# Two cross-attention layers on one core: queries of two units projected together in every second slot, and the second layer's weights loaded in six parts

## The chip, the cores and the metric

The kernel runs on one core of one Trainium2 chip. The metric is the device time of one execution in microseconds (us). A measurement of this kernel scatters by about 0.1% between runs (1834.97 to 1836.72 us in three runs).

## What is computed

Two grouped-query cross-attention layers one after the other, each on 32 batch entries of 112 query rows and 375 context rows, width 512, with 32 query heads over 8 key/value heads of 16 columns each:

```python
q = hidden_state @ Wq + bq          # [32, 112, 512]
k = encoder_hidden_state @ Wk + bk  # [32, 375, 128]
v = encoder_hidden_state @ Wv + bv  # [32, 375, 128]
scores = jnp.einsum('bkgld,bksd->bkgls', q, k) * scale + mask
attn = jax.nn.softmax(scores, axis=-1)
out = jnp.einsum('bkgls,bksd->bkgld', attn, v)   # back to [32, 112, 512]
x = out @ Wo + bo + hidden_state
x = (x - mean(x)) * rsqrt(var(x) + EPS) * gamma + beta
```

The second layer takes the first one's x, and the same context.

## The kernel before

A **unit** is one batch entry in one layer, so there are 64. Units run in two lines, p = 0 and p = 1 (even and odd batch entries), and the program is a chain of **slots** (p, i), i from -1 to 33, in the order (0, i), (1, i), (0, i+1). A slot works on five units at different stages: the scores, exponentials and values of its own unit (`main`), the row maxima and value projection of the next one of the other line (`ahead`), the end of the one before (`post`: reciprocals, output projection), the key and query projection of the next unit of its own line (`proj`), and the layer norm and store of the last one of its own line (`stored`).

A slot has 12 **pieces** (k = 0 to 11). Every piece has one pair of score matmuls on TensorE (tile `sc`, L741) and their two exponentials on ScalarE (ACT, L500); a `sc` buffer is written again only when its exponential is done. The other work of a slot hangs on the piece number, on each engine, by hand. On TensorE these are: 16 pairs of matmuls for the row maxima (tile `ms`, L758; `PAIRS_AT` says how many in which piece, one right behind the scores and the second, if there is one, at the piece's end), the values in two halves (tile `pv`, L777), the projections of values (L795), keys (L807), queries (L841) and outputs, a head in each of four pieces (L819), the transpose of the result rows in layer 0 (L832), and twice the small matmul that turns the maxima into rows (L786). VectorE (DVE) reduces each pair of `ms` to maxima (L627); there are two `ms` buffers, so pair j waits until pair j-2 is reduced:

```python
if j >= 2:
    pe.wait_ge(max_done[o], PAIRS * ahead + j - 1)
```

The maxima become three bf16 parts on POOL (L428 to L434), are turned by L786 into the tile `job`, copied by ACT (`mT`, L519) and brought by a DMA on SP's queue (L310) into the rows of `qs` from which the scores subtract them; the scores of piece 0 and piece 6 wait for these rows. `job` is one PSUM bank that values' projection, maxima's rows, queries and outputs take in turn, each waiting for the evacuation of the one before. Queries are projected by 16 matmuls of 112 columns for each unit, evacuated by four activations (L556), split into three bf16 parts by ACT and POOL, and stacked by 12 DMAs into `qs`.

TensorE, ACT, DVE and POOL work in program order; all loads, stacking and stores but the outputs' are issued in order on SP's queue (`slot` under `block.sync`). The second layer's weights (10 DMAs) are issued there at the end of slot (1, 1).

## Time and profile before

| | |
|---|---|
| Time, median of 3 runs | 1835.99 us |
| The profiled execution's own time | 1835.3 us |
| Its span in the profile | 1833.2 us |
| PE (TensorE) busy | 1779.6 us, 97% |
| DVE busy | 1370.1 us, 75% |
| ACT busy | 1078.4 us, 59% |
| POOL busy | 571.0 us, 31% |
| DMA, mean | 129 GB/s |

The profile's engines are PE for matmuls, PEld for the loads of stationary operands, DVE, ACT, POOL, and SP and ACT as issuers of DMAs (SPq, ACTq). An fp32 matmul has two records, a bf16 matmul one. A busy PE says that matmuls are in flight, not that each goes at its best rate, so distances from one start to the next are read rather than durations.

### The profile page before, as it was taken

What the parts mean: (1) busy time and instruction counts of PE and PEld (TensorE: products, weight loads), DVE (VectorE), ACT (ScalarE), POOL (GpSimd) and SP (SyncE); (2) the same over time, 40 slices, a digit from 0 to 9 for tenths busy, and PEclk for the clock granted to TensorE, in tenths of its full rate; (3) what the DMA queues carried; (4) which work ended last, traced back from release to release, by engine and by line L of the source; (5) the groups of instructions that cost most, each with busy time, mean ns of one, the idle gap of its engine ahead of it and who ended that gap; (6) DMA issues with size and microseconds to landing.
All of it is one profiled execution on the core that took longest, in us unless ns stands there. A gap on an engine that the chain in (4) does not pass through costs nothing. (4 is left out here: it accounts for less than half of the span.)

```text
span 1833.2 us, 37386 instructions
## 1 busy us (share of the span) xinstructions
PE 1779.6 (97%) x11521; PEld 1153.3 (63%) x11521; DVE 1370.1 (75%) x1808; ACT 1078.4 (59%) x2530; POOL 571.0 (31%) x1165
## 2 busy tenths in 40 slices
PE   4899999999999999999999999999999999999996
PEld 3566566666666666666666666666666666666652
DVE  6577677777777777777777777787777777777784
ACT  1465565666656656656656656656665656656653
POOL 1232233323323323323323323323323333333321
PEclk8899899999999999999999999999999999999997
DMA  8346445445445445445445445444444444444431
GB/s 288 100 121 180 130 125 137 129 120 140 129 121 139 132 117 142 133 115 144 133 119 144 128 109 135 128 111 133 128 114 131 126 116 127 125 126 117 129 82 42
DMA packets 200894, 235.92 MB, mean 129 GB/s; under 512 B 41706, under 2 KB 176100, under 8 KB 199812
## 3 DMA queue, kind: packets, MB, share of 16 engines
q1 hardware_dynamic: 180356, 205.82, 40.0%
q10 hardware_dynamic: 20480, 29.38, 6.9%
q8 instruction: 31, 0.51, 0.1%
q14 instruction: 27, 0.22, 0.0%
HBM read 101.39 MB, written 22.02 MB: 67 GB/s over the span
## 5 line engine op out<-in xcount | busy, mean ns | idle before, releaser
L627 DVE TENSOR_REDUCE mx<-ms 112x2 f32<-112x750 f32 x1024 | 933.4, 933 | 412.6 <-PE ms L758 401.1
L500 ACT ACTIVATE probs<-sc 125x448 f32<-125x448 f32 x1536 | 751.5, 542 | 344.5 <-PE sc L741 337.0
L758 PE MATMUL ms<-ks,qs 96*112 96x375 bf16 x2048 | 501.0, 326 | 10.4 <-DMA qs<-qp 7.8
L741 PE MATMUL sc<-qs,ks 99*125 99x448 bf16 x1536 | 423.6, 356 | 11.1 <-DMA qs<-mT 8.3
L758 PEld LDWEIGHTS ms<-ks,qs 96*112 96x112 bf16 x2048 | 254.7, 131 | 223.5 <-issue 114.4
L777 PE MATMUL pv<-probs,vs 125*32 125x448 f32 x3072 | 317.4, 546 | 0.0
L741 PEld LDWEIGHTS sc<-qs,ks 99*125 99x125 bf16 x1536 | 199.5, 138 | 127.5 <-ACT probs L500 75.3
L819 PE MATMUL job<-wo,on 128*112 128x512 f32 x512 | 268.6, 607 | 7.2 <-POOL on L442 5.7
L841 PE MATMUL job<-xT,wq 128*128 128x112 f32 x2048 | 249.9, 276 | 0.0
L841 PEld LDWEIGHTS job<-xT,wq 128*128 128x128 f32 x2048 | 245.2, 193 | 3.5 <-issue 0.6
L456 POOL TENSOR_TENSOR kr<-kf,kp 128x375 f32<-128x375 f32 x64 | 57.5, 899 | 534.5 <-ACT kp L537 534.5
L642 DVE RECIPROCAL orec<-osum 128x112 f32<-128x112 f32 x256 | 214.8, 841 | 5.8 <-DMA osum<-oraw 5.8
L807 PE MATMUL pv<-ctxT,wk 128*128 128x375 f32 x512 | 185.3, 484 | 10.0 <-DMA bq<-in_bq 10.0
L795 PE MATMUL job<-wv,ctxT 128*125 128x128 f32 x1536 | 191.9, 276 | 0.0
L795 PEld LDWEIGHTS job<-wv,ctxT 128*125 128x125 f32 x1536 | 187.7, 191 | 4.1
L777 PEld LDWEIGHTS pv<-probs,vs 125*32 125x32 f32 x3072 | 87.3, 110 | 163.1 <-issue 162.5
L508 ACT COPY oraw<-pv 128x448 f32<-128x448 f32 x128 | 68.1, 532 | 166.7 <-PE pv L777 166.7
L807 PEld LDWEIGHTS pv<-ctxT,wk 128*128 128x128 f32 x512 | 96.2, 192 | 49.0 <-issue 11.7
L556 ACT ACTIVATE qf<-job,bqs 128x112 f32<-128x112 f32 x256 | 69.6, 354 | 89.0 <-PE job L841 89.0
L428 POOL TENSOR_TENSOR mwide<-mx,zero 112x16 bf16<-112x16 f32 x128 | 27.5, 215 | 279.1 <-DVE mx L627 271.5
L475 POOL TENSOR_TENSOR qp<-qr,qp 128x224 bf16<-128x224 f32 x128 | 75.2, 608 | 104.9 <-ACT qp L574 104.9
L819 PEld LDWEIGHTS job<-wo,on 128*112 128x112 f32 x512 | 82.8, 178 | 37.1 <-issue 17.6
(54 smaller groups left out, 999.1 us busy)
## 6 DMA issues: line engine op xcount, KB each, us to landing
ctxT<-in_ctxT SPq DMA_DIRECT2D x64, 750.0 KB, 5.8
qs<-qp SPq DMA_DIRECT2D x768, 56.0 KB, 2.7
ks<-kp SPq DMA_DIRECT2D x768, 46.9 KB, 2.5
osum<-oraw ACTq DMA_DIRECT2D x128, 112.0 KB, 2.8
oc<-oraw ACTq DMA_DIRECT2D x128, 112.0 KB, 3.4
mask<-in_mask SPq DMA_DIRECT2D x64, 164.1 KB, 2.3
xT<-in_xT SPq DMA_DIRECT2D x32, 224.0 KB, 6.5
xin<-in_x SPq DMA_DIRECT2D x32, 224.0 KB, 6.6
```

Source lines behind the costliest of these rows:

```text
L475: nc.gpsimd.tensor_tensor(qp[:, 2, cols], qr[:, cols], qp[:, 1, cols], ALU.subtract)\
L500: nc.scalar.activation(probs[0:KCS, k, j, :], sc[j][0:KCS, 0:GL], ACT.Exp)\
L556: nc.scalar.activation(qf[:, S * c:S * c + S], job[:, S * c:S * c + S], ACT.Identity, bias=bqs[lay[3]][:, c:c + 1], scale=SCALE).then_inc( ...
L627: nc.vector.tensor_reduce(mx[o][:, 2 * j:2 * j + 2], ms[j % 2][0:S, :, 0:S2], AX_X, ALU.max)\
L642: nc.vector.reciprocal(orec[:, S * n:S * n + S], osum[:, S * n:S * n + S])\
L741: last = nc.tensor.matmul(sc[j][0:KCS, 0:GL], ks[p][0:KM, g, rows], qs[p][0:KM, g, :], start=True, stop=not masked)
L758: last = nc.tensor.matmul(ms[j % 2][0:S, n, 0:S2], qs[o][0:KT, g, S * c:S * c + S], ks[o][0:KT, g, :], start=True, stop=True)
L777: last = nc.tensor.matmul(pv[32 * j:32 * j + 32, 0:GL], vs[u][:, chunk, 4 * h + j, :, :].rearrange("s d two -> s (d two)"), probs[0:KCS, H ...
L795: last = nc.tensor.matmul(job[0:KCS, P * c:P * c + P], ctxT[o][:, t, KCS * c:KCS * c + KCS], wv[lay[1]][:, t, :], start=(t == 0), stop=(t ...
L807: last = nc.tensor.matmul(pv[:, 0:S2], wk[lay[3]][:, t, :], ctxT[p][:, t, :], start=(t == 0), stop=(t == DC - 1))
L819: last = nc.tensor.matmul(job[0:S, 0:D], on[:, S * c:S * c + S], wo[lay[2]][:, c, :], start=(c == 0), stop=(c == NG - 1))
L841: last = nc.tensor.matmul(job[:, S * c:S * c + S], wq[lay[3]][:, t, c, :], xT[p][:, t, :], start=(t == 0), stop=(t == DC - 1))
```

## The change

The place of every piece of work is now in tables with one row for p = 0 and one for p = 1. Queries of both units of a pair (same i, both lines) are projected in the slot of p = 0, by 16 matmuls of 224 columns for two units in place of 16 of 112 for each; `xT` holds both units side by side, `job` takes two heads' groups at a time, and ACT evacuates both units in one activation each group. In the slot of p = 0 two of the four heads' output projections move to the first two pieces of the slot of p = 1. Values' first half and the turned maxima come later in p = 0 (pieces 8 and 9 for 7 and 7). The store of the transposed rows moves a slot on, `xT` is loaded for both lines in the slot of p = 1, and the second layer's weights are loaded in six parts in slots (0,0), (1,0), (0,1), (1,1), (0,14) and (1,14).

```diff
-PAIRS_AT = [2, 2, 1, 2, 0, 1, 1, 1, 2, 2, 1, 1]
+PAIRS_AT = [[1, 1, 1, 1, 1, 1, 1, 2, 1, 2, 2, 2], [1, 1, 1, 1, 2, 1, 1, 1, 2, 2, 2, 1]]
+LATE_HEADS_AT = [{}, {0: (2,), 1: (3,)}]
+HEADS_AT = [{10: (0,), 11: (1,)}, {8: (0,), 9: (1,), 10: (2,), 11: (3,)}]
+KEYS_AT = [{2: (0,), 3: (1, 2), 4: (3,)}, {2: (0, 1), 3: (2, 3)}]
+VALUES_AT = [{1: (0, 1), 2: (2,)}, {4: (0, 1), 5: (2,)}]
+QUERIES_AT = [{4: (0,), 5: (1,), 6: (2,), 7: (3,)}, {}]
+COLUMNS_AT = [(9, 3), (7, 2)]
+FIRST_HALF_AT = [8, 7]
+RECIPROCALS_AT = [4, 4]
+WORK_FIRST = [(5,), (0,)]
...
-        xT = two(sb, "xT", [P, DC, S])
+        xT = sb("xT", [P, DC, PAR, S])
...
-                sp.dma_start(xT[p][:, :, :].rearrange("p a b -> p (a b)"), src[b]).then_inc(xT_in[p], 16)
+                sp.dma_start(xT[:, :, p, :], src[b].rearrange("p (a b) -> p a b", a=DC)).then_inc(xT_in[p], 16)
...
                     def project_queries(heads):
+                        if heads[0] % 2 == 0:
+                            take_job_bank()
                         if 0 in heads:
-                            take_job_bank()
-                            pe.wait_ge(xT_in[p], 16 * (proj + 1))
+                            for u in range(PAR):
+                                pe.wait_ge(xT_in[u], 16 * (proj + 1))
                         for c in heads:
                             for t in range(DC):
-                                last = nc.tensor.matmul(job[:, S * c:S * c + S], wq[lay[3]][:, t, c, :], xT[p][:, t, :],
+                                last = nc.tensor.matmul(job[:, PAR * S * (c % 2):PAR * S * (c % 2 + 1)], wq[lay[3]][:, t, c, :],
+                                                        xT[:, t, :, :].rearrange("p u l -> p (u l)"),
                                                         start=(t == 0), stop=(t == DC - 1))
...
+            def next_layer(p, i):
+                if (p, i) == (0, 0):
+                    load_wk(1, w_in[1])
+                    load_wv(1, w_in[1])
+                if (p, i) == (1, 0):
+                    load_wq(1, w_in[1], slice(0, 2))
+                if (p, i) == (0, 1):
+                    load_wq(1, w_in[1], slice(2, DC))
+                if (p, i) == (1, 1):
+                    load_wo(1, w_in[1], slice(0, 2))
+                if (p, i) == (0, PER - 2):
+                    load_wo(1, w_in[1], slice(2, NG))
+                if (p, i) == (1, PER - 2):
+                    load_rows(1, w_in[1])
```

Three places in the built programs. First TensorE, pieces 5 to 7 of a slot of p = 0 before the change: scores (L741), a pair for the maxima (L758), queries (L841) in two blocks of eight matmuls, and the transposes between.

```order
L741 MATMUL sc<-qs,ks 125x448 x2
L753 REGISTER_ALU
L758 MATMUL ms<-ks,qs 112x375 x2
L841 MATMUL job<-xT,wq 128x112 x8
L738 ISA
L741 MATMUL sc<-qs,ks 125x448 x2
L753 REGISTER_ALU
L758 MATMUL ms<-ks,qs 112x375 x2
L832 MATMUL pv<-ident,y 128x112 x4
L841 MATMUL job<-xT,wq 128x112 x8
```

The same engine at the same place of the changed program (scores L834, maxima L851, queries L937, transposes L925), from the end of piece 5 to piece 7:

```order
L937 MATMUL job<-xT,wq 128x224 x4
L846 REGISTER_ALU
L851 MATMUL ms<-ks,qs 112x375 x2
L831 ISA
L834 MATMUL sc<-qs,ks 125x448 x2
L846 REGISTER_ALU
L851 MATMUL ms<-ks,qs 112x375 x2
L925 MATMUL pv<-ident,y 128x112 x4
L822 ISA
L937 MATMUL job<-xT,wq 128x224 x4
```

Blocks of eight narrow matmuls became blocks of four matmuls twice as wide, one in each of pieces 4 to 7; the slot of p = 1 has none.

Second TensorE again, the changed program's pieces 8 to 10 of p = 0, with the values' first half (L870), the turned maxima (L879) and the first head of the output projection (L912):

```order
L870 MATMUL pv<-probs,vs 32x448 x12
L831 ISA
L834 MATMUL sc<-qs,ks 125x448 x2
L846 REGISTER_ALU
L851 MATMUL ms<-ks,qs 112x375 x2
L822 REGISTER_ALU
L878 ISA
L879 MATMUL job<-negident,mwide 128x112
L846 REGISTER_ALU
L851 MATMUL ms<-ks,qs 112x375 x2
L831 ISA
L834 MATMUL sc<-qs,ks 125x448 x2
```

Piece 9 now holds no projection between its scores and those of piece 10; before, the turned maxima stood right behind the values, and each of the pieces 8 to 11 had a head.

Third SP's queue, the end of slot (1, 1) before the change, with the ten loads of the second layer's weights in one go:

```order
L299 DMA yT_mid<-yT 128x448
L364 DMA wk<-in_Wk 128x512
L365 DMA bk<-in_bk 128x1
L368 DMA wq<-in_Wq 128x2048
L369 DMA bq<-in_bq 128x4
L372 DMA wv<-in_Wv 128x512
L361 DMA bv<-in_bv 125x128
L376 DMA wo<-in_Wo 128x2048
L361 DMA bo<-in_bo 112x512
L361 DMA gamma<-in_gamma 112x512
L361 DMA beta<-in_beta 112x512
```

And the middle of slot (1, 0) in the changed program, with one of the six parts:

```order
L330 DMA qs<-mT 3x16x112
L298 DMA xT<-in_xT 128x4x112 x2
L399 DMA wq<-in_Wq 128x1024
L308 DMA xin<-in_x 112x512
L325 DMA ks<-kp 16x4x375 x6
L285 DMA ctxT<-in_ctxT 128x1500
L325 DMA qs<-qp 16x4x448 x5
L330 DMA qs<-mT 3x16x112
```

The part stands behind the slot's first row of maxima (L330) and ahead of `xin`, the stacking of the keys and, in a slot of p = 1, the context, which moved behind the keys' stacking.

## Rows read from the trace of the kernel before

**Rows 1.** The page, busy time by engine (us, share, instructions)
```profile
PE 1779.6 (97%) x11521; PEld 1153.3 (63%) x11521; DVE 1370.1 (75%) x1808; ACT 1078.4 (59%) x2530; POOL 571.0 (31%) x1165
```

**Rows 2.** Timeline of PE in a layer-0 slot (start, length, line, operation, records)
```profile
804.64 0.55 PE L741 MATMUL sc<-qs,ks 99*125 99x448 bf16 x2
805.02 0.48 PE L758 MATMUL ms<-ks,qs 96*112 96x375 bf16 x2
805.52 1.11 PE L819 MATMUL job<-wo,on 128*112 128x512 f32 x2
806.46 0.49 PE L758 MATMUL ms<-ks,qs 96*112 96x375 bf16 x2
806.78 0.54 PE L741 MATMUL sc<-qs,ks 99*125 99x448 bf16 x2
807.16 0.48 PE L758 MATMUL ms<-ks,qs 96*112 96x375 bf16 x2
807.48 1.02 PE L819 MATMUL job<-wo,on 128*112 128x512 f32 x2
808.34 0.48 PE L758 MATMUL ms<-ks,qs 96*112 96x375 bf16 x2
...
816.04 1.91 PE L795 MATMUL job<-wv,ctxT 128*125 128x128 f32 x16
817.78 0.49 PE L758 MATMUL ms<-ks,qs 96*112 96x375 bf16 x2
...
824.37 1.94 PE L841 MATMUL job<-xT,wq 128*128 128x112 f32 x16
826.14 0.55 PE L741 MATMUL sc<-qs,ks 99*125 99x448 bf16 x2
```

**Rows 3.** Timeline of PE, values' first half (piece 7) of successive slots, layer 0
```profile
129.35 2.46 PE L777 MATMUL pv<-probs,vs 125*32 125x448 f32 x24
156.89 2.46 PE L777 MATMUL pv<-probs,vs 125*32 125x448 f32 x24
193.89 2.46 PE L777 MATMUL pv<-probs,vs 125*32 125x448 f32 x24
```

**Rows 4.** The same in layer 1
```profile
1240.47 2.46 PE L777 MATMUL pv<-probs,vs 125*32 125x448 f32 x24
1267.69 2.46 PE L777 MATMUL pv<-probs,vs 125*32 125x448 f32 x24
```

**Rows 5.** Timeline of ACT around the pieces 8 and 9 of Rows 2
```profile
804.71 0.53 ACT L508 COPY oraw<-pv 128x448 f32<-128x448 f32 x1 [0.46 <-PE pv L777]
805.14 0.24 ACT L519 CAST mT<-job 48x112 bf16<-48x112 f32 x1
...
807.17 0.54 ACT L500 ACTIVATE probs<-sc 125x448 f32<-125x448 f32 x1 [0.38 <-PE sc L741]
...
807.61 0.54 ACT L500 ACTIVATE probs<-sc 125x448 f32<-125x448 f32 x1
```

**Rows 6.** Timeline of DVE, the reduction behind the maxima's pair at 805.02
```profile
805.55 0.94 DVE L627 TENSOR_REDUCE mx<-ms 112x2 f32<-112x750 f32 x1 [1.56 <-PE ms L758]
```

**Rows 7.** Timeline behind the second layer's weight loads, SP's queue and PE
```profile
180.49 0.78 SPq L310 DMA_DIRECT2D qs<-mT  x1
...
187.55 1.00 PE L741 MATMUL sc<-qs,ks 99*125 99x448 bf16 x2 [6.61 <-DMA qs<-mT]
```

**Rows 8.** The page, DMA issues (count, KB each, median us from issue to landing)
```profile
ctxT<-in_ctxT SPq DMA_DIRECT2D x64, 750.0 KB, 5.8
qs<-qp SPq DMA_DIRECT2D x768, 56.0 KB, 2.7
...
xT<-in_xT SPq DMA_DIRECT2D x32, 224.0 KB, 6.5
```

**Rows 9.** Timeline of PE at the start, from the first maxima to the first scores
```profile
32.38 1.47 PE L758 MATMUL ms<-ks,qs 96*112 96x375 bf16 x4 [5.68 <-DMA qs<-qp]
...
55.45 1.01 PE L741 MATMUL sc<-qs,ks 99*125 99x448 bf16 x2 [1.32 <-DMA qs<-mT]
```

More of the change, by code:

```diff
@@ L327, in slot @@
                     max_rows(p, 1, count(2 * main + 2))
+                turned = stored if p == 1 else stored - 1
+                if not isinstance(turned, int) and lay[4] == 0 or isinstance(turned, int) and 0 <= turned < PER:
+                    store_yT(o, turned)
                 if s_ok:
                     store_y(p, stored, lay[4])
-                if more and not (isinstance(ahead, int) and ahead + 1 == 0):
-                    after = lay[3] if not isinstance(ahead, int) else 0 if ahead + 1 < PER else 1
-                    load_ctx(o, ahead + 1, after)
-                    load_xT(o, ahead + 1, after)
+                if p == 1 and (not isinstance(proj, int) or 0 < proj + 1 < UNITS):
+                    after = lay[3] if not isinstance(proj, int) else 0 if proj + 1 < PER else 1
+                    for u in range(PAR):
+                        load_xT(u, proj + 1, after)
+                if isinstance(i, int):
+                    next_layer(p, i)
+                if more and p == 0 and not (isinstance(ahead, int) and ahead + 1 == 0):
+                    load_ctx(o, ahead + 1, lay[3] if not isinstance(ahead, int) else 0 if ahead + 1 < PER else 1)
                 if m_ok:
@@ L384, in _ @@
             load_xT(0, 0, 0)
+            load_xT(1, 0, 0)
             for n in range(BLOADS):
@@ L519, in m_out, with k_out, q_out, rows_out @@
                     nc.scalar.copy(mT[:, :], job[0:PARTS * HH, 0:S]).then_inc(mt_evac[u], 1)
+                def k_out():
+                    act.wait_ge(k_ps[p], proj + 1)
+                    if a_ok:
+                        act.wait_ge(k_r[o], ahead + 1)
+                    if m_ok:
+                        act.wait_ge(stack[p][0], 16 * NSTACK * (main + 1))
+                        act.wait_ge(stack[p][1], 16 * NSTACK * (main + 1))
+                    nc.scalar.activation(kf[:, :], pv[:, 0:S2], ACT.Identity, bias=bk[lay[3]][:, 0:1])\
+                      .then_inc(k_evac[p], 1)
+                    act.wait_ge(k_evac[p], proj + 1)
+                    nc.scalar.copy(kp[p][:, 0, :], kf[:, :]).then_inc(k_p1[p], 1)
+                def q_out(heads):
+                    act.wait_ge(q_ps, 2 * proj + heads[-1] // 2 + 1)
+                    if heads[0] == 0:
+                        for u in range(PAR):
+                            need(act, q_r[u], 2 * proj)
+                    for c in heads:
+                        nc.scalar.activation(qf[:, :, S * c:S * c + S],
+                                             job[:, PAR * S * (c % 2):PAR * S * (c % 2 + 1)].rearrange("p (u l) -> p u l", u=PAR),
+                                             ACT.Identity, bias=bqs[lay[3]][:, c:c + 1], scale=SCALE).then_inc(q_evac, 1)
+                def rows_out():
+                    act.wait_ge(t_ps[p], stored + 1)
+                    if not isinstance(stored, int) or 2 * stored + p > 0:
+                        need(act, yT_out[o], 16 * (stored + p))
+                    nc.scalar.copy(yT[:, :, :].rearrange("p a b -> p (a b)"), pv[:, 0:GL])\
+                      .then_inc(yT_ready[p], 1)
                 for k in range(PIECES):
@@ L679, in slot @@
                             dve.wait_ge(mask_in[o], 16 * (ahead + 1))
[L680 to L683 removed]
+                        for step in range(max(PAIRS_AT[p][k], 1)):
+                            if a_ok and step < PAIRS_AT[p][k]:
+                                maximum(PAIR0[p][k] + step)
+                            if k == RESIDUAL_AT[p] and step == 0 and s_ok:
                                 residual()
```

254 lines of the change are left out of this document (134 added, 120 removed).

## Prediction

> **What bounds the kernel now.** I read the page first, for the busy shares: PE 97%, DVE 75%, ACT 59% [rows 1]. A busy PE alone says little, so next came PE's timeline of one slot [rows 2]. The reader is to see there that each block starts where the block before it lets it: scores at 806.78, maxima at 807.16, a head at 807.48, maxima again at 808.34, with no gap that another engine causes. One small wait stands out. From the maxima at 805.02 to the first head is 0.50 us and the head takes 0.94, where the next head comes 0.32 behind its maxima and takes 0.86: (0.50 + 0.94) - (0.32 + 0.86) = 0.26 us lost in each slot, because the first head needs the bank `job` that ACT's copy at 805.14 has to empty [rows 2, 5]. So in the steady part the time is the sum of TensorE's blocks. A slot is 156.89 - 129.35 = 27.54 us in layer 0 [rows 3] and 1267.69 - 1240.47 = 27.22 us in layer 1, which has no transposes [rows 4]; 64 such slots are most of the span. The third view is the same timeline where a slot is longer than that: one takes 193.89 - 156.89 = 37.00 us [rows 3], and in it the scores waited 6.61 us for a row of maxima whose DMA was issued at 180.49, behind the second layer's weights, and was in use at 187.55 only [rows 7]. The fourth is the start, where PE waits too [rows 9].
>
> **The queries.** A block of eight matmuls of 112 columns takes 826.14 - 824.37 = 1.77 us, and a block of eight of 128 columns 817.78 - 816.04 = 1.74 us [rows 2]. Fewer columns are not cheaper, so the columns are not what these two wait for. A head of 512 columns takes 0.86 us, one of 128 takes 1.74 / 8 = 0.218. The trace has no 224 columns. By the line between those two rows, (0.86 - 0.218) / 384 = 1.67 ns a column, a matmul of 224 columns takes 0.218 + 96 x 0.00167 = 0.378 us. The bounds: at worst it costs twice a narrow one, 0.442, and nothing is gained; at best it costs what 224 columns cost at the 512-column rate, 224 x 1.68 ns = 0.376. I take 0.378, since the wide rows leave no room for a fixed cost. A pair of slots had four blocks, 7.08 us; it now has 16 x 0.378 = 6.05. The gain is 1.03 us a pair.
>
> The block of 112 columns has 16 loads of weights in 1.77 us, 0.111 us each. The Trainium skill (TensorE: Matmul & The Clock Gate, LDWEIGHTS) puts a load at its number of columns over 1.2, which is 107 ns for 128 columns, and says in Back-to-back issue gap that load and stream set the spacing together; the trace agrees to 4%. By its figure of 107 ns the narrow block would be load-bound and the wide one, at twice the stream, would not, so its estimate of the gain would be the same 1.0 us a pair.
>
> **Waits that go or come inside a pair of slots.** I laid the changed order of TensorE out with the distances above and looked at each piece for what its first instruction needs.
>
> The first head's wait of 0.26 us goes in p = 0, since ACT's copy of the maxima now stands a piece ahead of the head. It stays in p = 1. Gain 0.26.
>
> Piece 9 of p = 0 becomes short: scores, a pair for the maxima, the turned maxima, a pair, and nothing else. At 0.38 + 0.32 + 0.06 + 0.32 it is 1.09 us (the 0.06 is an estimate for 112 bf16 columns, at a quarter of the fp32 rate of 1.67 ns a column). Two things are late for piece 10. The reduction of the piece's first pair starts 0.53 us behind its matmuls and takes 0.94 [rows 2, 6], so it ends 0.38 + 0.53 + 0.94 = 1.85 us into the piece, and piece 10's first pair, which needs that buffer, would stand at 1.09 + 0.38 = 1.47: it waits 0.4. ACT first copies `pv` (0.53 from the start of the piece, the next operation follows 0.43 behind [rows 5]), so the second exponential ends near 0.07 + 0.43 + 0.44 + 0.54 = 1.48 at the earliest, where the second score matmul wants its buffer at 1.28. This 0.2 lies inside the 0.4. Loss 0.4 a pair.
>
> Piece 6 of p = 1 has in layer 0 scores, a pair and transposes, in layer 1 scores and a pair only. The length in layer 1 is 0.38 + 0.32 = 0.70. An exponential starts 0.39 behind its scores, the second 0.44 later, and ends after 0.54 more: 1.37 us [rows 2, 5]. The second score matmul of piece 7 wants its buffer at 0.70 + 0.19 = 0.89. So it waits 0.5 us in layer 1, and, with 0.32 more in the piece, 0.15 in layer 0. Before, this piece had a block of queries that covered it. What is late next is nothing: piece 7 has the values, 2.4 us.
>
> So a pair gains 1.03 + 0.26 - 0.4 - 0.15 = 0.74 us in layer 0, and 1.03 + 0.26 - 0.4 - 0.5 = 0.39 in layer 1. Queries are projected in 31 pairs of slots with scores, 15 in layer 0 and 16 in layer 1: 11.1 + 6.2 = 17.3 us.
>
> **Other engines.** The two slots become unequal. p = 1 loses 3.54 us of queries and gets two heads, 1.72: 27.54 - 1.82 = 25.7 us. DVE's work of a slot is 1370.1 / 64 = 21.4 us at most [rows 1], but in p = 1 its first pair stands behind a head and the values (0.38 + 0.86 + 2.4 = 3.64 us), so DVE has 25.7 - 4.2 = 21.5 us from there to the slot's end. That is just enough, and what is left over runs into the next slot, whose maxima need it 0.4 us later. I cost it at nothing; the price if it fails is a rival below. ACT's activations for queries are half as many, hidden by PE both ways.
>
> **The loads.** The long slot loses 37.00 - 27.54 = 9.46 us to the weights. In six parts, the largest is 512 KB against the context's 750 KB, which lands in 5.8 us [rows 8] and stands in every slot; each part stands behind the slot's first row of maxima, and the next one is needed more than 8 us later. I take the full 9.5 us.
>
> `xT` is now written in runs of 448 bytes, where it had 1792. Its load took 6.5 us [rows 8]. It is issued in p = 1 after the result rows and needed in piece 4 of the next p = 0, some 25 us later; it would have to take four times as long to be missed. I cost it at nothing. The Trainium skill (DMA: Bandwidth & Descriptors, Specifications) asks for 512 bytes or more a run for full rate, which speaks against this layout. No row here shows the price of shorter runs, and the distance of 25 us covers a fourfold time (26 us) all but for 1 us.
>
> **The start.** The first slot projects both units while it waits anyway: its queries grow by 2.5 us inside a wait of 5.68 us [rows 9], though evacuation and splitting then start later, at the cost of up to half a us. The second slot loses its two blocks (2 x 1.77 = 3.54 us) and its maxima come sooner, so that the row of maxima for which the first scores wait (1.32 us) may be there in time: 3.54 + 1.32 - 0.4 = 4.5 us. The bounds are 0 (DVE or the stacking sets the first scores' time) and 4.9. In the tail nothing changes that I can see.
>
> **Sum.** 17.3 + 9.5 + 4.5 = 31.3 us off the profiled execution's own 1835.3 us gives 1804.0. The median, 1836.0, is 0.7 above that execution, so the forecast for a median is 1804.7; I give 1805. Its own range is 1795 to 1815, mostly for the start and for the two short pieces. A measurement of this kernel can tell about 0.2%, 3.7 us, from no change.
>
> **Rivals.** *No stalls.* The short pieces cost nothing, because my distances add up latencies that overlap. Then the pairs give 31 x 1.29 = 40 us, the sum is 54, and the time 1782. For it: in the slot of Rows 2 nothing waits. Against it: the reduction's own 0.94 us is longer than the room it has. Chance 0.17.
>
> *DVE becomes the bound in p = 1.* If its chain of maxima is a little longer than the 21.5 us it has, each pair loses the difference. With 0.5 to 0.8 us the time is 1805 + 31 x 0.65 = 1825. For it: the room above is 0.1 us. Against it: 21.4 us counts work of the start and both layers over 64 slots, and the last pair of a slot may run over. Chance 0.15.
>
> *The row of maxima comes late in p = 0* (slower). It is turned in piece 9 now. From that piece's start to the next slot's scores are 1.09 + 0.4 + 2 x 1.88 = 5.3 us (a piece with a head and two pairs is 0.38 + 0.32 + 0.86 + 0.32 = 1.88). ACT's copy ends at 1.5 + 0.24, and with the 2.7 us of the stacking DMAs [rows 8] the row is there at 4.5. Slack 0.8 us, where there were three heads more before. If SP's queue or the DMAs are late by more than that, each us costs one a pair; at 1.0 us beyond the slack the whole gain is gone, at 2.0 the time is 1804 + 62 = 1866. For it: the wait in [rows 7] is this very wait. Against it: that one stood behind 3 MB of weights. Chance 0.06.
>
> *The wide matmuls gain nothing*, at 0.442 us each: 1805 + 31 x 1.03 = 1837, no change. The straight line through 128 and 512 columns speaks against it. Chance 0.03.
>
> *xT comes late*, if short runs take over four times as long, as the page's rule on short runs would have it at its worst: at 8 us in place of 6.5 nothing shows; at 28 us each pair waits 3 us and the time is 1805 + 93 = 1898. The queue's stores of 896-byte rows into `qs` land in 2.7 us [rows 8], against it. Chance 0.02.
>
> **How the numbers follow.** The forecast has 0.57. Faster by over 0.2%: 0.57 + 0.17 + nearly all of 0.15 gives 0.88; within 0.2%: 0.05; slower: 0.07. The range takes the forecast's own, the case without stalls and most of DVE's: 1782 to 1824.
>
> **What would show it.** In the changed profile a block of four query matmuls should stand 1.51 us ahead of what follows; DVE should be named as the releaser of maxima in piece 10 of p = 0 with about 0.4 us, ACT as that of scores in piece 7 of p = 1; pairs of slots should be near 54.3 us in layer 0 and 54.1 in layer 1; no slot of 37 us; first scores near 51. The prediction is wrong if pairs come out at 53.8 or below (no stalls), if PE waits for DVE through p = 1, or if scores of piece 0 wait for `mT`'s DMA.

## The result, and the profile after

The changed kernel takes 1827.64 us (median of 7 runs, 1824.91 to 1831.58), the kernel before 1836.68 us in the same session (7 runs, 1834.97 to 1837.59). The ratio is 0.9952, with a 95% interval of 0.9942 to 0.9961: 9.0 us faster, where 31 were forecast. The profiled span went from 1833.16 to 1824.45 us, 8.72 less before rounding; the readings below account for these 8.7.

The page of the changed kernel, busy time by engine, costliest groups and DMA issues (as in [rows 1] and [rows 8]):

```profile
span 1824.4 us, 35260 instructions
PE 1767.7 (97%) x10497; PEld 1105.2 (61%) x10497; DVE 1353.9 (74%) x1808; ACT 1049.0 (57%) x2402; POOL 588.9 (32%) x1165
...
L937 PE MATMUL job<-xT,wq 128*128 128x224 f32 x1024 | 216.2, 354 | 0.9 <-ACT qf L624 0.9
...
ctxT<-in_ctxT SPq DMA_DIRECT2D x64, 750.0 KB, 6.2
...
xT<-in_xT SPq DMA_DIRECT2D x32, 224.0 KB, 3.7
```

The shares hardly moved. What tells is again the distance from one start to the next. The timeline of PE, values' first half (L870) of p = 0 in one pair and in the next, in layer 0 and in layer 1; the two rows of each layer are two slots apart:

```profile
184.63 2.46 PE L870 MATMUL pv<-probs,vs 125*32 125x448 f32 x24
239.42 2.46 PE L870 MATMUL pv<-probs,vs 125*32 125x448 f32 x24
...
1394.70 2.46 PE L870 MATMUL pv<-probs,vs 125*32 125x448 f32 x24
1449.20 2.46 PE L870 MATMUL pv<-probs,vs 125*32 125x448 f32 x24
```

A pair takes 54.79 us in layer 0 and 54.50 in layer 1. Read the same way over two slots, the kernel before takes 55.30 in layer 0 (55.10 in the last pairs of it) and 54.50 in layer 1. So a pair gains 0.52 us in layer 0 and nothing at all in layer 1, where 0.74 and 0.39 were forecast. The slot of 37 us is gone.

Where the 8.7 us are is seen by the first scores of each slot of p = 0, which stand at the same place of both programs. They are at 55.45 us before and 54.57 after in slot (0,0), at 231.17 and 218.50 in (0,3), 839.46 and 821.11 in (0,14), 949.73 and 936.33 in (0,16), 1767.64 and 1755.49 in (0,31):

| stretch | forecast, us | measured, us |
|---|---|---|
| to the first scores of (0,0) | -4.5 | -0.88 |
| (0,0) to (0,3): three pairs and the burst of weights | -11.7 | -11.79 |
| (0,3) to (0,14): eleven pairs of layer 0 | -8.1 | -5.68 |
| (0,14) to (0,16): two pairs, the layers' boundary | -1.1 | +4.95 |
| (0,16) to (0,31): fifteen pairs of layer 1 | -5.9 | +1.25 |
| (0,31) to the end | 0 | +3.43 |
| sum | -31.3 | -8.72 |

The first row is one profile of each kernel, and the start scatters: `rows_early` below, the same program up to slot (1,1), has its first scores at 56.64 us, and `split_only` and `split_late`, which start as the kernel before does, at 56.50 and 56.95. So the start's gain is known to some 2 us only.

The waits of PE in the changed kernel, from its list of waits (for whom; us in total, times, longest):

```profile
PE sc L834 <- DMA qs<-mT: 6.0, 5, 1.6
...
PE ms L851 <- DVE mx L726: 4.4, 9, 1.1
...
PE sc L834 <- ACT probs L584: 3.9, 20, 0.3
PE sc L834 <- issue: 2.5, 1, 2.5
```

Scores that wait for a row of maxima (`qs<-mT`) happened twice outside the burst before, one of them at the start; now five slots have it (1.59 us at the start, 1.57, 1.41, 0.84 and 0.61), and a sixth wait, of 2.5 us, has no name ("issue"). SP's queue ahead of one of them, and PE:

```profile
99.67 0.53 SPq L285 DMA_DIRECT2D ctxT<-in_ctxT  x1
100.24 3.10 SPq L325 DMA_DIRECT2D qs<-qp  x5
103.39 0.77 SPq L330 DMA_DIRECT2D qs<-mT  x1
...
108.90 0.59 PE L834 MATMUL sc<-qs,ks 99*125 99x448 bf16 x2 [1.57 <-DMA qs<-mT]
```

In a slot of p = 1 the row of 10.5 KB is now issued behind the context's 750 KB, and 5.51 us pass from its issue to the scores that use it. By the semaphore updates in the trace the row landed 5.47 us behind its issue. For this row the median from issue to landing over all slots of p = 1 is 3.7 us, where it was 2.2 before the change; for its like in slots of p = 0 it is 2.2 in both kernels. That line of the diff (`load_ctx` behind the keys' stacking for p = 1) the prediction left uncosted.

**The short piece 9 of p = 0.** The timeline of PE, ACT and DVE there, in layer 1:

```profile
1397.09 0.59 PE L834 MATMUL sc<-qs,ks 99*125 99x448 bf16 x2
1397.52 0.49 PE L851 MATMUL ms<-ks,qs 96*112 96x375 bf16 x2
1397.84 0.21 PE L879 MATMUL job<-negident,mwide 112*128 112x112 bf16 x1
1397.89 0.48 PE L851 MATMUL ms<-ks,qs 96*112 96x375 bf16 x2
1398.26 0.84 PE L834 MATMUL sc<-qs,ks 99*125 99x448 bf16 x2
1399.03 0.53 PE L851 MATMUL ms<-ks,qs 96*112 96x375 bf16 x2
...
1397.65 0.99 ACT L584 ACTIVATE probs<-sc 125x448 f32<-125x448 f32 x2
...
1398.04 2.63 DVE L726 TENSOR_REDUCE mx<-ms 112x2 f32<-112x750 f32 x3 [2.15 <-PE ms L851]
```

Scores take 0.38 us to what follows; those at 1398.26 take 0.77. DVE's first reduction is over at 1398.04 + 0.94 = 1398.98, and the maxima that need its buffer start 0.05 later. ACT's second exponential ends at 1398.64, in the middle of the scores, and the second score matmul starts 0.05 us behind that, 0.25 late. The 0.39 us is there as forecast, some 0.25 behind ACT and the rest behind DVE, though the list of waits names nobody for it.

**The short piece 6 of p = 1**, PE and ACT:

```profile
1416.44 0.54 PE L834 MATMUL sc<-qs,ks 99*125 99x448 bf16 x2
1416.83 0.48 PE L851 MATMUL ms<-ks,qs 96*112 96x375 bf16 x2
1417.49 0.84 PE L834 MATMUL sc<-qs,ks 99*125 99x448 bf16 x2 [0.18 <-ACT probs L584]
1418.17 0.48 PE L851 MATMUL ms<-ks,qs 96*112 96x375 bf16 x2
...
1416.90 0.98 ACT L584 ACTIVATE probs<-sc 125x448 f32<-125x448 f32 x2 [0.54 <-PE sc L834]
```

From 1416.44 to 1417.49 is 1.05 us where 0.70 of work stands, and the second scores take 0.68 where 0.38 is their length. That is 0.65 us, where 0.5 was forecast; in layer 0 it is 0.25 where 0.15 was. The second exponential ends at 1417.88, and the maxima stand 0.29 behind it.

### The profile page after: what moved, and what is told of

Read it like the earlier page. It is cut to its first block and busy times, and to the rows that moved or that the text cites. A ratio compares the mean times of both kernels' runs of the same rounds, so it can differ in the third digit from the quotient of the medians.

```text
span 1824.4 us, 35260 instructions
## 1 busy us (share of the span) xinstructions
PE 1767.7 (97%) x10497; PEld 1105.2 (61%) x10497; DVE 1353.9 (74%) x1808; ACT 1049.0 (57%) x2402; POOL 588.9 (32%) x1165
## 2 busy tenths in 40 slices
DMA packets 225756, 235.89 MB, mean 129 GB/s; under 512 B 74506, under 2 KB 200708, under 8 KB 224932
## 5 line engine op out<-in xcount | busy, mean ns | idle before, releaser
L851 PE MATMUL ms<-ks,qs 96*112 96x375 bf16 x2048 | 499.0, 327 | 8.5 <-DVE mx L726 4.4
L834 PE MATMUL sc<-qs,ks 99*125 99x448 bf16 x1536 | 441.6, 360 | 14.8 <-DMA qs<-mT 6.0
L851 PEld LDWEIGHTS ms<-ks,qs 96*112 96x112 bf16 x2048 | 256.9, 130 | 211.9 <-issue 78.6
L870 PE MATMUL pv<-probs,vs 125*32 125x448 f32 x3072 | 319.2, 549 | 0.0
L834 PEld LDWEIGHTS sc<-qs,ks 99*125 99x125 bf16 x1536 | 193.5, 136 | 178.2 <-ACT probs L584 73.0
L912 PE MATMUL job<-wo,on 128*112 128x512 f32 x512 | 267.0, 604 | 7.1 <-POOL on L493 5.7
L937 PE MATMUL job<-xT,wq 128*128 128x224 f32 x1024 | 216.2, 354 | 0.9 <-ACT qf L624 0.9
L741 DVE RECIPROCAL orec<-osum 128x112 f32<-128x112 f32 x256 | 214.5, 840 | 0.9 <-DMA osum<-oraw 0.9
L900 PE MATMUL pv<-ctxT,wk 128*128 128x375 f32 x512 | 190.9, 485 | 11.2 <-DMA bq<-in_bq 11.2
L937 PEld LDWEIGHTS job<-xT,wq 128*128 128x128 f32 x1024 | 190.0, 189 | 15.3 <-ACT qf L624 4.3
L870 PEld LDWEIGHTS pv<-probs,vs 125*32 125x32 f32 x3072 | 87.4, 110 | 181.2 <-issue 168.4
L497 POOL TENSOR_TENSOR kr<-kf,kp 128x375 f32<-128x375 f32 x64 | 72.8, 1138 | 346.1 <-ACT kp L615 346.1
L517 POOL TENSOR_TENSOR rstd<-veps,neghalf 112x1 f32<-112x1 f32 x64 | 36.4, 569 | 258.3 <-DVE veps L759 258.3
L912 PEld LDWEIGHTS job<-wo,on 128*112 128x112 f32 x512 | 85.6, 178 | 29.6 <-ACT mT L603 11.7
L493 POOL TENSOR_TENSOR on<-oc,orec 128x224 f32<-128x224 f32 x128 | 84.4, 659 | 56.3 <-DVE orec L741 54.5
```

Of the source, the lines that this page charges most:

```text
L493: nc.gpsimd.tensor_tensor(on[:, cols], oc[:, cols], orec[:, cols], ALU.mult).then_inc(on_ready[o], 1)
L497: nc.gpsimd.tensor_tensor(kr[:, :], kf[:, :], kp[p][:, 0, :], ALU.subtract).then_inc(k_r[p], 1)
L741: nc.vector.reciprocal(orec[:, S * n:S * n + S], osum[:, S * n:S * n + S])\
L834: last = nc.tensor.matmul(sc[j][0:KCS, 0:GL], ks[p][0:KM, g, rows], qs[p][0:KM, g, :], start=True, stop=not masked)
L851: last = nc.tensor.matmul(ms[j % 2][0:S, n, 0:S2], qs[o][0:KT, g, S * c:S * c + S], ks[o][0:KT, g, :], start=True, stop=True)
L870: last = nc.tensor.matmul(pv[32 * j:32 * j + 32, 0:GL], vs[u][:, chunk, 4 * h + j, :, :].rearrange("s d two -> s (d two)"), probs[0:KCS, H ...
```

## Experiments

All times are medians, compared with the kernel before on the same chip (1835.8 to 1836.2 us in the three sessions). The changed kernel's 1827.64 us come from another session, in which the kernel before took 1836.68, so a difference from it of under 1 us says nothing. Pairs of slots are read as above.

### The loads alone

`split_only` is the kernel before with the six parts of the second layer's weights, each behind the slot's first row of maxima and ahead of the context, as in the change. `split_late` issues the same parts as the last thing in each slot's list. Both also take over the change's later place of VectorE's wait for these weights. The diff of `split_only`, without the functions that load the parts:

```diff
                     store_y(p, stored, lay[4])
+                if isinstance(i, int):
+                    next_layer(p, i)
                 if more and not (isinstance(ahead, int) and ahead + 1 == 0):
...
-                if isinstance(i, int) and (p, i) == (1, 1):
-                    load_wk(1, w_in[1])
-                    load_wq(1, w_in[1])
-                    load_wv(1, w_in[1])
-                    load_wo(1, w_in[1])
```

> The kernel before with the second layer's weights loaded in the same six parts and slots as in the changed kernel, and nothing else of the change. If the queries' part of the change nets to nothing, because its gain in layer 0 is eaten at the start, at the layers' boundary and by late rows of maxima, this kernel alone gives about 9 us less than before, near 1827, as the whole change does: the slot of 37.0 us becomes one of 27.6. If its boundary between the layers also shows a wait of some 2.5 us with a slow stretch behind it, the parts loaded last cause that wait by themselves, and the time is nearer 1831; if the boundary shows none, the wait needs the new order of SP's queue or the queries. A rival, that the burst's cost only moves to the six slots, would give 1836.

Measured: 1831.56 us (10 runs), ratio 0.9971 (0.9962 to 0.9981), 4.6 us faster and not 9.5. The number is near the 1831 of the expectation, but not by its reason: the pair at the boundary between the layers takes 55.21 us and shows no wait. The pair that had the burst takes 55.09 us, so the burst is gone. But a new wait stands earlier, at the first scores of slot (1, 0):

```profile
80.68 0.78 SPq L310 DMA_DIRECT2D qs<-mT  x1
...
86.34 0.56 PE L760 MATMUL sc<-qs,ks 99*125 99x448 bf16 x2 [2.63 <-DMA qs<-mT]
```

The row was 5.66 us from its issue to its use (landed after 5.56), behind a part of 512 KB and the context. Its pair takes 57.88 us in place of 54.19. So 3.7 of the 9.5 us that the burst cost are only moved; the first scores of this profile also stand 1.05 us later, which is within the start's scatter.

> The kernel before with the second layer's weights in six parts, each issued at the end of its slot's work on SP's queue and not ahead of the context. It is the loads' part of the change alone, without the wait of 2.6 us that the parts ahead of the context brought to slot (1,0) when nothing else was changed. If a burst of 9.5 us is all that the loads were worth, the time is 1827 (no slot over 27.7 us behind the start). A rival, that the DMA engines' time for 3 MB must be paid somewhere, leaves some slots longer and gives 1830 or more. Against the changed kernel with the context loaded last (1818.8) it tells what the queries' part is worth: 8 us by the pairs of layer 0 (15 x 0.52) and nothing in layer 1.

Measured: 1833.41 us, ratio 0.9985 (0.9975 to 0.9994). The pair of the burst takes 55.11 us, and the rows of maxima are in time, but the first scores of layer 1 wait for the last part, and their pair takes 60.30 us in place of 55.17:

```profile
885.22 0.43 SPq L359 DMA_DIRECT2D beta<-in_beta  x1
...
889.91 0.59 PE L760 MATMUL sc<-qs,ks 99*125 99x448 bf16 x2 [3.36 <-DMA beta<-in_beta]
```

All engines wait at the start of layer 1 for all twelve loads. A load spread over the whole layer still has its last part, and that one had a deadline 4.7 us away. The time is in the rival's range (1830 or more), but what is paid is this one late part, not the DMA engines' time for 3 MB: no other slot grew by it.

### The boundary between the layers, and the context's place

`rows_early` is the changed kernel with the last part (three rows of 224 KB) issued in slot (1,1) and no longer in (1,14):

```diff
                     load_wo(1, w_in[1], slice(0, 2))
+                    load_rows(1, w_in[1])
...
-                if (p, i) == (1, PER - 2):
-                    load_rows(1, w_in[1])
```

> The changed kernel with the last part of the second layer's weights (bo, gamma, beta, three rows broadcast over 112 partitions) loaded in slot (1,1) behind the first half of wo and not in slot (1,14). Theory: these three loads keep the DMA engines full while the row of maxima for the first slot of layer 1 is stacked, and TensorE waits for both; without them the pair of slots at the boundary falls from 59.0 us to about 54.8 and the time from 1827.6 to about 1823.5. Rival: the wait there comes from the order of SP's queue alone (context and five stacking DMAs ahead of the row of maxima); then the boundary keeps more than 57 us and the time is 1827.

Measured: 1828.75 us, ratio 0.9961 (0.9946 to 0.9976), no faster than the changed kernel. The pair at the boundary takes 54.65 us in place of 58.99, so without this part it costs nothing. Other rows of maxima came later instead: one wait of 2.50 us at 168.65 and one of 1.64 at 1101.66, where the changed kernel had 0.84. Moving one load moves the wait; the slot's own queue is too full ahead of the row.

`context_last` leaves the loads where the change put them, and issues the context of p = 1 behind the row of maxima and the last stacking:

```diff
                     stack_terms(p, 0, ks[p], kp[p], 1)
-                if more and p == 1 and not (isinstance(ahead, int) and ahead + 1 == 0):
-                    load_ctx(o, ahead + 1, lay[3] if not isinstance(ahead, int) else 0 if ahead + 1 < PER else 1)
...
                     stack_terms(p, 0, qs[p], qp, 0, of=(2,))
+                if more and p == 1 and not (isinstance(ahead, int) and ahead + 1 == 0):
+                    load_ctx(o, ahead + 1, lay[3] if not isinstance(ahead, int) else 0 if ahead + 1 < PER else 1)
```

> The changed kernel with the load of the context in slots of p = 1 issued behind the row of maxima and the last stacking DMA, where it stood ahead of the queries' stacking. Theory: the row of maxima lands late because 750 KB go ahead of it; the waits of scores for it (1.57, 1.41, 0.84 and 0.61 us in the profiled run) go, the spread of the times (1824.9 to 1831.6) narrows to that of the kernel before, and the median is 3 to 5 us lower, near 1823. Rival: the five stacking DMAs of 0.62 us each ahead of it in SP's queue are what delays it; then the waits stay and the time is 1827.

Measured: 1818.8 us (4 runs), ratio 0.9905 (0.9889 to 0.9922), 8.8 us faster than the changed kernel. Pairs of slots are unchanged, 54.78 and 54.50 us. The pair at the boundary takes 54.65 us, and in the steady part no score waits for `mT` any more. The same slot as above, SP's queue and PE:

```profile
103.74 0.77 SPq L330 DMA_DIRECT2D qs<-mT  x1
104.56 0.59 SPq L325 DMA_DIRECT2D qs<-qp  x1
105.26 0.55 SPq L285 DMA_DIRECT2D ctxT<-in_ctxT  x1
...
106.41 0.54 PE L834 MATMUL sc<-qs,ks 99*125 99x448 bf16 x2
```

The row is issued no earlier (103.74 and 103.39), but it is there within 2.67 us in place of 5.51; its median over the slots of p = 1 falls from 3.7 to 2.5 us. So it was late by its transfer, behind the context's bytes, and not by its place in the list of issues. The waits at 108.90, at the boundary and behind it have one cause, then, and the change itself brought it. At the boundary the changed kernel's wait names no releaser, but the trace tells:

```profile
876.11 0.16 DVE L713 TENSOR_SCALAR bqs<-bq 128x4 f32<-128x4 f32 x1
...
878.45 0.93 PE L834 MATMUL sc<-qs,ks 99*125 99x448 bf16 x2 [2.52 <-issue]
```

DVE's L713 waits for all twelve loads of the second layer's weights and runs at 876.11 us, so they were there by then. The row of maxima was issued at 872.87 and landed at 878.36, 0.09 us ahead of the scores. The row ended this wait too. It stood behind the context and, before that, the last part, which is why taking away either load removes the wait.

### The width of the query matmuls

`narrow` is the changed kernel with 8 matmuls of 112 columns in each block in place of 4 of 224:

```diff
-                            for t in range(DC):
-                                last = nc.tensor.matmul(job[:, PAR * S * (c % 2):PAR * S * (c % 2 + 1)], wq[lay[3]][:, t, c, :],
-                                                        xT[:, t, :, :].rearrange("p u l -> p (u l)"),
+                            for u in range(PAR):
+                                at = PAR * S * (c % 2) + S * u
+                                for t in range(DC):
+                                    last = nc.tensor.matmul(job[:, at:at + S], wq[lay[3]][:, t, c, :], xT[:, t, u, :],
```

> The changed kernel with the queries of two units still in the slot of p = 0 and in the same pieces, but by 8 matmuls of 112 columns a block in place of 4 of 224. It measures what the wide matmuls alone give. Theory (width is what gains, and the short pieces 9 of p = 0 and 6 of p = 1 keep what they cost, because no query work lies near them): a block takes 1.77 us in place of 1.51, four blocks 1.04 us more a pair, so pairs of slots are near 55.8 us in layer 0 and 55.5 in layer 1, longer than before the change (55.1 to 55.3 and 54.5), and the time is 1827.6 + 31 x 1.0 = 1860. Rival (part of the wide matmuls' gain is taken away by the short pieces only because everything came sooner, so that it comes back as fewer waits): pairs near 55.3 and 55.0, the time 1842 to 1848.

Measured: 1852.9 us, ratio 1.0088 (1.0072 to 1.0103). Pairs take 55.82 us in layer 0 and 55.53 in layer 1, so width is worth 1.04 and 1.03 us a pair, as the line through two rows of the trace had it, and all of it arrives. The new order of the pieces by itself costs 0.52 us a pair in layer 0 and 1.03 in layer 1. The time is 7 us below the theory's. In the profiled execution (1856.7 us, the slowest of the four) the waits for `mT` fall differently, none at 108.9 and a pair of 56.93 at the boundary, which makes 3 us; the other 4 lie between this execution and the median, and no trace shows them.

### The two short pieces

`values_spread` is the changed kernel with the values' projection of p = 1 in pieces 4, 5 and 6, so that piece 6 has a block of 0.87 us:

```diff
-VALUES_AT = [{1: (0, 1), 2: (2,)}, {4: (0, 1), 5: (2,)}]
+VALUES_AT = [{1: (0, 1), 2: (2,)}, {4: (0,), 5: (1,), 6: (2,)}]
```

> The changed kernel with the value projection of a slot of p = 1 in pieces 4, 5 and 6, one chunk each, and not two chunks in piece 4 and one in piece 5. Piece 6, which in layer 1 holds only scores and a pair of maxima, gets 0.87 us of cover. Theory: piece 7's wait for the exponentials (0.34 before the scores and 0.30 inside them in layer 1) goes, so pairs of slots fall from 54.5 to about 53.9 us in layer 1 and from 54.8 to about 54.5 in layer 0: 16 x 0.64 + 15 x 0.25 = 14 us, time near 1814. Rival: the reduction of the maxima on VectorE sets the length of the slots of p = 1, and the wait only moves to a later piece; then pairs and time stay within 2 us of 1827.6.

Measured: 1831.45 us, ratio 0.9981 (0.9969 to 0.9992). This fell: pairs are 55.32 us in layer 0 (0.54 longer) and 54.56 in layer 1. These pairs alone would cost 0.54 x 15 + 0.06 x 16 = 9 us; the time grew by 3.8 only, since rows of maxima come late elsewhere: in this profile the pair at the boundary takes 55.61 us in place of 59.0, and nothing waits at the first scores of (0,1). The wait left piece 7 and came back in the scores of pieces 5 and 6 (0.58 us each) and ahead of piece 6 (0.30). PE and ACT at piece 6:

```profile
1419.72 0.74 PE L834 MATMUL sc<-qs,ks 99*125 99x448 bf16 x2
...
1418.48 0.65 ACT L660 CAST qp<-qf 128x224 bf16<-128x224 f32 x2
...
1419.04 0.97 ACT L584 ACTIVATE probs<-sc 125x448 f32<-125x448 f32 x2
```

The casts of the queries, which the change put into piece 4 of p = 1, hold up ACT's exponentials there, and a piece of 1.57 us no longer hides them.

`cl_casts_late` takes `context_last` and moves these casts, and the stacking behind them, to piece 6 and later. GpSimd's and SP's order follow (not shown), so that three stacking DMAs and not five stand ahead of the first row of maxima in p = 1, as before the change:

```diff
-QUERY_PARTS_AT = [7, 4]
+QUERY_PARTS_AT = [7, 6]
```

> The changed kernel with the context loaded last, and with the first casts of the queries in p = 1 moved on ScalarE from piece 4 to piece 6 (the second ones to piece 8), GpSimd's and SP's order following. Theory: spreading the values did not help because ScalarE's own queue from piece 3 to piece 6 of p = 1 (copies of keys, a cast that waits for GpSimd, two casts of queries, four pieces of exponentials) sets when piece 7's scores may start, not the shortness of piece 6. With 0.65 us less in it the waits of 0.64 us in layer 1 and 0.25 us in layer 0 nearly go: pairs of 53.9 and 54.5 us, 16 x 0.6 + 15 x 0.25 = 13 us, time near 1806 against 1818.8. Rival: piece 6's shortness (0.7 us against the 1.3 us of two exponentials and their start) sets it by itself; then the wait stays at 0.5 us in layer 1 and the gain is under 4 us.

Measured: 1818.02 us, ratio 0.9898 (0.9882 to 0.9915), pairs unchanged at 54.78 and 54.50 us. At the short piece nothing moved: the exponentials start 0.66 us after ACT was free, and PE waits as before.

```profile
1407.03 0.55 PE L830 MATMUL sc<-qs,ks 99*125 99x448 bf16 x2
...
1407.48 0.98 ACT L580 ACTIVATE probs<-sc 125x448 f32<-125x448 f32 x2 [0.66 <-PE sc L830]
1408.08 0.13 PEld L830 LDWEIGHTS sc<-qs,ks 99*125 99x125 bf16 x1 [0.53 <-ACT probs L580]
1408.08 0.84 PE L830 MATMUL sc<-qs,ks 99*125 99x448 bf16 x2 [0.18 <-ACT probs L580]
```

So ACT's load is not what PE waits for there. It is the round from scores to exponential and back, 1408.08 - 1407.03 = 1.05 us for the first buffer, which a piece of 0.70 cannot cover.

`cl_head_nine` takes `context_last`, gives piece 9 of p = 0 a head and turns the maxima in piece 8:

```diff
-LATE_HEADS_AT = [{}, {0: (2,), 1: (3,)}]
-HEADS_AT = [{10: (0,), 11: (1,)}, {8: (0,), 9: (1,), 10: (2,), 11: (3,)}]
+LATE_HEADS_AT = [{}, {1: (3,)}]
+HEADS_AT = [{9: (0,), 10: (1,), 11: (2,)}, {8: (0,), 9: (1,), 10: (2,), 11: (3,)}]
...
-COLUMNS_AT = [(9, 3), (7, 2)]
+COLUMNS_AT = [(8, 3), (7, 2)]
```

> The changed kernel with the context loaded last in slots of p = 1, and with three heads of the output projection in pieces 9, 10 and 11 of p = 0 and one late (piece 1 of p = 1), the turned maxima in piece 8. Piece 9 is no longer short. Theory: the wait of 0.39 us inside piece 10's scores goes, the first head's wait of 0.17 and the slower first head (0.09) come back in p = 0, so a pair of slots gains about 0.2 us (54.5 to 54.3 in layer 1, 54.8 to 54.6 in layer 0), 6 us in all: 1813 against 1818.8. Rival: the exponentials behind the copy of pv are what is late, wherever the head stands, so the wait only moves to piece 9 or 10, and the time stays at 1818.

Measured: 1809.03 us, ratio 0.985 (0.9834 to 0.9867), pairs 54.53 and 54.25 us, 0.25 less in both layers. Over 31 pairs that is 7.8 of the 9.8 us by which it is below `context_last`; both numbers speak against the rival. `cl_both` has both edits:

> The changed kernel with the context loaded last, the three heads in pieces 9 to 11 of p = 0, and the casts of the queries in p = 1 late. If both theories hold the gains add: pairs near 53.7 us in layer 1 and 54.3 in layer 0, time near 1800. If VectorE then sets the slots of p = 1, which would be 25.4 us long against its 21.5 us of work behind the first pair, less than the sum is seen, and the waits are for the reduction of the maxima.

Measured: 1809.11 us, ratio 0.9855 (0.9839 to 0.9871), pairs 54.53 and 54.25: nothing on top, in agreement with `cl_casts_late`.

`cl_three` is `cl_both` with the values' edit of `values_spread`:

> The kernel with the context's load behind the maxima's row, a head in piece 9 of p = 0 and the queries' casts late, and now also the last block of the values' projection in piece 6 of p = 1 (blocks in pieces 4, 5, 6 in place of 4, 4, 5). Theory: the wait in piece 7 of p = 1 comes from the piece being short, and when its cover was moved there alone the casts of the queries on ACT in piece 4 held the exponentials of pieces 4 and 5; with the casts in piece 6 and later the pieces 4 and 5 are free, so both waits go: pairs near 54.2 us in layer 0 and 53.7 in layer 1, the time near 1800. Rival: pieces 4 and 5 with one block each are themselves short enough that the next score matmuls wait for their exponentials, or DVE holds the maxima there; then pairs stay at 54.2 or more in layer 1 and the time stays at 1808 to 1810.

Measured: 1805.43 us (5 runs, 1801.65 to 1805.82), ratio 0.9822 (0.9808 to 0.9835). Pairs are 53.81 us in layer 1, 0.44 less, and 54.57 in layer 0, 0.04 more. PE and ACT at the places that `values_spread` had spoiled:

```profile
1396.12 0.74 PE L830 MATMUL sc<-qs,ks 99*125 99x448 bf16 x2
...
1397.90 0.54 PE L830 MATMUL sc<-qs,ks 99*125 99x448 bf16 x2
...
1399.22 0.66 ACT L656 CAST qp<-qf 128x224 bf16<-128x224 f32 x2
1399.48 0.54 PE L830 MATMUL sc<-qs,ks 99*125 99x448 bf16 x2
```

In layer 1 the scores of pieces 6 and 7 follow in 0.38 us, only those at 1396.12 still take 0.59. So two edits that each gave nothing or lost (the casts: 0; the values: -0.06) give 0.44 us a pair together: the cover for the round to ACT, and an ACT that is free in the pieces from which the cover was taken. In layer 0, where the old wait was 0.25 us, the waits that came back (0.20 in the scores of piece 5, 0.12 at the maxima of piece 7) eat the gain, as the rival says. This kernel is the fastest of the study, 22 us below the changed one. That it takes the 1805 us of the forecast is chance: it has four edits that the forecast kernel has not.

## Why the prediction was wrong

The forecast was 1805 us and the range 1782 to 1824; the time is 1827.64. The direction was right, 9 us of 31 came, and 22.6 us are missing by the profiles. The steps that failed are four. Rows of maxima that come late in p = 1, which the sum had at nothing, cost 8.9 us (`context_last` against the changed kernel, from slot (0,0) to (0,31)). The pairs gave 6.7 us less than forecast: the same stretch of `context_last` is 20.1 us shorter than before the change, where 26.8 were forecast. The start gave 3.6 less, the end, also at nothing, cost 3.4. My own sign of being wrong, scores of piece 0 that wait for `mT`'s DMA, is what the first of these shows. Term by term:

**The queries' width: right.** 1.03 us a pair forecast; the block of the changed kernel takes 1.51, in one place of four 1.61, and `narrow` shows 1.03 and 1.04. Against the kernel before, the blocks on their own sum to 7.08 - 6.15 = 0.93 in layer 1. The second estimate there, from the 107 ns a load of the Trainium skill (TensorE: Matmul & The Clock Gate, LDWEIGHTS), comes to 64 x 0.107 - 6.05 = 0.80 us and not to the 1.0 that I gave; the sum does not use it.

**The short piece 9: right.** 0.4 forecast, 0.39 read. `cl_head_nine` gave back 0.25 of it in each pair; a head there costs some of its own.

**The short piece 6 of p = 1: mechanism right, size too small.** 0.5 forecast in layer 1 and 0.65 read, 0.15 and 0.25 in layer 0. I laid the end of the second exponential against the start of the second scores, but the first scores of the piece wait too (0.35), and the second then wait for the second exponential anew (0.30).

**The first head's wait: too large by 0.09.** 0.26 was to go in p = 0; 0.17 went, since the head that moved to piece 0 of p = 1 takes 0.95 to what follows and not 0.86.

**A cost without a term.** The scores behind each half of the values take 0.43 us where they took 0.38, twice a pair, 0.10 us. What causes it I did not test.

These give 0.93 + 0.17 - 0.39 - 0.65 - 0.10 = -0.04 in layer 1, where 0.00 was measured, and with 1.06 for the blocks and 0.25 for piece 6 they give 0.49 in layer 0, where 0.52 was measured. Over 15 and 16 steady pairs the shortfall from the forecast would be 0.22 x 15 + 0.39 x 16 = 9.5 us. It is 6.7, mostly because the first pair is another case: it took 55.88 us before and 53.25 in `context_last`, and two waits for stacking DMAs (1.18 us at 57.63 and 0.93 at 84.52) went with the change. I had no term for that.

**The burst: right by itself.** 9.46 forecast and 9.24 read (the pair of 64.54 us against 55.30). What failed is the step beside it, "each part stands behind the slot's first row of maxima, and the next one is needed more than 8 us later". The time to the next row's need says nothing of how long that row's own transfer takes when it is issued behind a part and a context. I also read "the context, which moved behind the keys' stacking" in the order of SP's queue and gave it no price. `split_only` shows the first effect in the kernel before (3.7 us in one pair), `context_last` the second: 8.9 us, the waits at 108.90, the boundary and behind it. I had the mechanism as a rival, but only for p = 0, by the slack of the turned maxima, while the queue had changed for p = 1.

**The start: step failed.** 4.5 us forecast and 0.88 came, near the lower of the bounds that I gave, which named DVE or the stacking. It was the stacking. The timeline of the start, with SP:

```profile
46.95 0.21 PE L879 MATMUL job<-negident,mwide 112*128 112x112 bf16 x1 [1.99 <-POOL mwide L485]
...
47.20 0.25 ACT L603 CAST mT<-job 48x112 bf16<-48x112 f32 x1 [1.91 <-PE job L879]
...
47.65 0.53 SPq L285 DMA_DIRECT2D ctxT<-in_ctxT  x1
48.23 3.98 SPq L325 DMA_DIRECT2D qs<-qp  x5
...
52.25 0.84 SPq L330 DMA_DIRECT2D qs<-mT  x1
...
54.57 1.01 PE L834 MATMUL sc<-qs,ks 99*125 99x448 bf16 x2 [1.59 <-DMA qs<-mT]
```

The first maxima come no sooner (32.78 us against 32.38 in [rows 9]), the turned ones stand 2.2 us earlier, but the row is issued 4.8 us after ACT has copied it, behind the context and five stacking DMAs, and then takes the usual 2.3 us. SP's queue sets this chain. The stacking of the keys starts 3.66 us sooner (43.77 us for 47.43, with the keys now projected ahead of the values), but from there to the row's issue the queue takes 8.48 us where it took 5.71, since the context and two stackings more stand ahead of the row. I took 3.54 us of PE's work off a chain that PE does not set; these two lines of the queue had no term. `context_last` gets its first scores at 54.72, so the context alone does not hold them. `cl_casts_late`, `cl_both` and `cl_three` have the two stackings behind the row again, issue it 6.1 to 6.7 us behind the start of the keys' stacking and get the first scores at 53.27, 53.75 and 53.88; with the scatter of the start (above) this points the same way and is not more than that.

**The end: a step that I had at nothing.** It costs 3.43 us, and 3.1 of them lie in slot (0,31), 26.8 us long where it was 23.7. It has no queries, and PE waits there; in `context_last` it is as long (26.7), so the late rows are not the reason. The windows of the changed kernel (PE, PEld, DVE, ACT, POOL busy, then the granted clock):

```profile
1762.00:1767.60 5.60, 4.78 (x26) 2.59 (x24) 4.95 (x7) 4.10 (x11) 0.00 (x0) 1.00 0.13 35
1769.50:1776.20 6.70, 5.59 (x27) 1.98 (x30) 4.91 (x7) 0.98 (x2) 2.14 (x6) 0.50 0.06 21
```

Its scores wait 0.61 us for a row at 1766.54, its maxima 0.51 us for DVE at 1768.98 and 1.11 at 1770.62. The clock falls between the last two: from 1769.4 to 1776.2 us it is at 0.50, 1.2 GHz, and the values' half at 1772.88 takes 4.09 us where it takes 2.46 at 2.4 GHz. In the kernel before the same slot has full clock to its end, 1.00 from 1780.80 to 1791.30, and falls to 0.78 and 0.54 only in the slot behind it, in which both kernels are slow. The boundary between the layers has the same pair: a wait of 2.52 us and then 1.2 GHz from 878.5 to 881.9 us, some 1.5 us of work more. The wait and the half clock make 4.0 of the 4.2 us by which that pair is too long. `context_last` tests this for the boundary: it takes the wait away, and the clock stays at 1.00 from 60.8 to 1749 us. Which waits bring the clock down stays open. It fell to 0.50 for 3.4 us within 1.6 us of the end of waits of 2.63 us (`split_only`, 86.34), 3.36 (`split_late`, 889.91), 1.64 (`rows_early`, 1101.66) and 1.84 (`values_spread`, 1103.23), but not behind one of 2.50 (`rows_early`, 168.65), of 1.83 (`narrow`, 1116.67) or of 1.57 (the changed kernel, 108.90). For the end no run took the waits away.

**The rivals.** "DVE becomes the bound in p = 1" gives 1825, near the time, but that is luck: in the steady part no maxima of p = 1 wait for DVE, and `cl_three` goes on to 53.81 us a pair with DVE's work the same. "No stalls" fell. "xT comes late" fell: its load takes 3.7 us where it took 6.5. (The fourfold time in this rival is its room of 25 us over 6.5; the rule that it leans on, cited below, names no factor.) The load stands elsewhere in the queue, ahead of the context's, so the two figures do not price the short runs. The Trainium skill (DMA: Bandwidth & Descriptors, Specifications) asks for 512 bytes a run; packets under that rose from 41706 to 74506, and no run here shows a price of them.

## What to carry to other kernels

A change that takes work out of an engine which is busy all the time gains what the work took only where its neighbours stay long enough for the round trips beside them: count, for each piece that becomes short, the round to the engine that empties its buffer, for both buffers. When transfers are moved, price the small and urgent one that is issued behind a large one; put the large one behind it, and look at each slot kind apart. A cover and a clear queue may be needed together, so two edits that give nothing alone are worth one run in common.

## What the runs showed of the hardware

In slots of p = 1 a DMA of 10.5 KB took 3.7 us in the median and up to 5.5 from issue to landing behind a load of 750 KB on the same queue (the changed kernel), and 2.5 in the median, 3.7 at most, ahead of it (`context_last`). At one place with the same time of issue (103.4 and 103.7 us) it was in use after 5.51 and after 2.67 us. I had counted only the place in the list.

A matmul of 224 fp32 columns takes 1.51 / 4 = 0.378 us to the next, exactly the line between 128 and 512 columns, while 112 and 128 columns cost the same.

Behind five single waits of 1.64 to 3.36 us in an otherwise full PE the granted clock was at 0.50 for 3.4 us, and the pair of slots grew by 1.4 to 2.1 times the wait: by 4.2 us for 2.52 in the changed kernel, by 3.5 for 1.64 in `rows_early`. Behind others of up to 2.50 us it stayed at 1.00, and there the pair grew by 1.1 to 1.2 times the wait (3.0 us for 2.50 in `rows_early`, 2.0 for 1.83 in `narrow`).
